# Attention and feed-forward steps on one core: ScalarE's squares put ahead of VectorE's rotation, and the Gelu, its table loads and the copies of a step reordered

## The chip, the cores and the metric

The program runs on one core of a Trainium2 chip. The metric is the device time of one execution in microseconds (us); lower is better. It is given as the median of several runs, and one further execution was taken by the profiler.

## The reference, cut to what matters

Eight sequences of 256 tokens with 128 features go through six layers of local attention and a gated feed-forward. A linear attention branch is computed once ahead of them, and the two are combined at the end. What the change touches is inside one layer:

```python
qkv = x @ Wqkv                       # 16 heads of 64
q = l2norm(q) * qs ; k = l2norm(k) * ksc
q = q * cos * scale + rotate_half(q) * sin * scale
k = k * cos * inv   + rotate_half(k) * sin * inv
sim = einsum(q, k over own and previous window of 32) * 8, masked
attn = softmax(sim) ; out = attn @ v ; x = out @ Wo + x
xn = layernorm(x) ; a, gate = split(xn @ W1 + b1)
x = (a * gelu(gate)) @ W2 + b2 + x
...
g = silu(x) ; result = x_in + s * g
```

## The kernel before, in words

The five engines run five programs written out by hand, in order, and meet at semaphores. The work is cut into 48 **steps** (`n`, one sequence of one layer) and each step into 4 **units** (`u = 4 n + j`, with `j` from 0 to 3: two groups of eight heads by two tiles of 128 tokens). The `j`-th part of a step is called **slot j** here. An iteration of the loop is software-pipelined: slot j of step n projects unit u, turns q and k of unit u-2, scores them and takes their softmax, multiplies unit u-3 with v, and does a share of the feed-forward of the sequences n-1, n-2 and n-3. Steps 0 to 2 and the three after the last are written out; the others are a loop on each engine. The same program body serves all, with `live(...)` leaving out what does not exist.

What each engine does in one slot, in its order (before the change):

- **TensorE** (lines 727 to 764): project q (three matmuls, lines 617 to 619, by the helper line 490), turn q of u-2 into `ps_qs` (line 596), project k, turn k into `ps_tk`, project v, in slot 2 the down projection `ff_down` (line 711 on), turn the probabilities of u-3 into `ps_po` (`turn_p`, line 604), the scores of u-2 (`scores`, line 621: one matmul with the mask, then 64 small ones; it waits for both `q_turned` and `k_turned`), a share of out projection or `ff_up`, and the values of u-3. A projection into `ps_q` or `ps_k` waits until the last reader of that bank is done. `ff_down` waits for `xn_ready` of the next sequence, since both use the bank `ps_f`; `ff_up` of chunk 0 waits for `x_ready`, which `after_ff` gives.
- **ScalarE** (lines 918 to 953): `keep_turned` copies q and then k out of PSUM (through the helper line 838), `squares_of` squares q and k (line 844; it waits until VectorE has rotated them), `keep_p` copies the turned probabilities in two halves, `start_norms` takes Ln and Exp of the sums of squares (lines 876 and 878), `ff_copy` takes the up projection (lines 899 and 901), then the Exp of the softmax (line 944), `keep_v` and `keep_attention`. At the end of slot 0 stands the Gelu of sequence n-3 (line 906), ahead of which the compiler puts a load of the activation table; in slot 1 `natural_log_exp_and_others` is loaded back (line 935). In the last steps `silu_start` (line 914) takes an Exp of a finished sequence, at the end of a slot.
- **VectorE** (lines 1188 to 1229): `rotate` q and `rotate` k (two tensor_tensor from PSUM each, lines 1076 and 1078), with `ln_normalise` (line 1153, gives `xn_ready`) between them in slot 2, then the two sums of squares (line 1084), `clamp` (line 1094, a tensor_scalar of 18 columns), in slot 2 `after_ff` (line 1159), `find_max` (line 1116), `newton_1` (line 1099), `less_max` (line 1121, gives `sub_done`, for which the Exp waits), `newton_2` and `newton_3` (lines 1105 and 1111), and `sums` (lines 1127 and 1130). In slot 3 `newton_2`, `newton_3` and `after_attention` (line 1135) stand ahead of `less_max`. In the last steps `silu` (lines 1173 to 1187: a chain of six operations on VectorE for a finished sequence) ends a slot.
- **GpSimd** (lines 462 to 481): `divide` for u-3 (line 433), `add_halves` for q and k (line 418, waits for each rotation), in slot 1 the gate `ff_gate` (lines 440 and 442), in slot 2 the split of a slice of weights, in slot 3 the rounding of x, then `normalise` q and k (line 426, waits for `rnorm_done` from `newton_3`).
- **SyncE** issues the loads of the weights and the shifted copies of v.

The squares and the rotation both read the projection in its PSUM bank. Before the change their order is rotation, then squares:

```python
            def squares_of(u, i, s):
                wait(act, ssq_done, 2 * (u - 2) + i + 1)
                act.wait_ge((q_scaled, k_scaled)[i], u + 1)
```

```python
                wait(dve, (tq_done, tk_done)[i], u - 1)
                wait(dve, added, u - 1)
                dve.wait_ge(done, u + 1)
```

Of the kernel before, what the change touches and what calls it, by code (L numbers as in the profile page):

```python
# [39 lines left out]
UNITS = 4  # L40
# [22 lines left out]
def build(nc, x, wq, wk, wv, wp, bp, conv_w, conv_b, wqkv, q_scale, k_scale, wo, ln_g, ln_b, w1, b1, w2,  # L63
          rotary, masks, eye, head_block, out):
    with ExitStack() as ctx:
# [422 lines left out]
        def _(pe):  # L488
# [238 lines left out]
            def body(n):  # L727
                for j in range(UNITS):
                    u = UNITS * n + j
                    for i, ps, free, done in ((0, ps_q, q_squared, q_done), (1, ps_k, k_squared, k_done)):  # L730
                        if live(u):
                            project(n, j, i, ps, free, done)

                        if live(u - 2):
                            turn_qk(u - 2, i, j % 2)
                        if i == 1 and j == 0 and live_batch(n - 2):
                            ln_mean(n - 2)
                        if i == 0 and j == 1 and live_batch(n - 2):
                            ln_variance(n - 2)
                        if i == 0 and j == 2 and live_batch(n - 2):  # L740
                            ln_spread(n, n - 2)
                        if i == 0 and j == 3 and live_batch(n - 2):
                            ff_up(n - 2, 1)
# [26 lines left out]
        def _(act):  # L770
# [69 lines left out]
            def squares_of(u, i, s):  # L840

                wait(act, ssq_done, 2 * (u - 2) + i + 1)
                act.wait_ge((q_scaled, k_scaled)[i], u + 1)
                nc.scalar.activation(squares[:, s, OCTET * i:OCTET * i + OCTET], (ps_q, ps_k)[i][:], ACT.Square  # L844
                                     ).then_inc((q_squared, k_squared)[i], 1)
# [8 lines left out]
            def keep_turned(u, j, s):  # L854

                octet, tile = j // 2, j % 2
                wait(act, s_done, u - 1)
                act.wait_ge(tq_done, u + 1)
                copy(q_t[:, s, :], ps_qs[:]).then_inc(q_turned, 1)
                act.wait_ge(tk_done, u + 1)  # L860
                copy(k_t[:, octet, :, WINDOW + P * tile:WINDOW + P * tile + P],
                     ps_tk[:].rearrange("p (c t) -> p c t", t=P)).then_inc(k_turned, 1)
# [55 lines left out]
            def body(n):  # L918
                for j in range(UNITS):
                    u = UNITS * n + j  # L920
                    if live(u - 2):
                        keep_turned(u - 2, (j - 2) % UNITS, j % 2)
                    if live(u):
                        squares_of(u, 0, j % 2)
                    if j == 0 and live(u - 3):
                        keep_p(u - 3, (j - 3) % 2)
                    if live(u):
                        squares_of(u, 1, j % 2)
                    if j > 0 and live(u - 3):
                        keep_p(u - 3, (j - 3) % 2)  # L930
# [11 lines left out]
                    if live(u - 2):  # L942
                        act.wait_ge(sub_done, u - 1)
                        nc.scalar.activation(prob[:, j % 2, :], prob[:, j % 2, :], ACT.Exp,  # L944
                                             scale=QK_SCALE).then_inc(exp_done, 1)
                    if live(u):
# [3 lines left out]
                    if j == 0 and live_batch(n - 3):  # L950
                        gelu(n - 3)
                    for b in silu_at(n, j):
                        silu_start(b)
# [5 lines left out]
        def _(dve):  # L959
# [104 lines left out]
            def rotate(n, j, i):  # L1064
# [4 lines left out]
                ps, done, scaled, added = ((ps_q, q_done, q_scaled, q_added), (ps_k, k_done, k_scaled, k_added))[i]  # L1069
                wait(dve, (tq_done, tk_done)[i], u - 1)  # L1070
                wait(dve, added, u - 1)
                dve.wait_ge(done, u + 1)
# [116 lines left out]
            def body(n):  # L1189
                for j in range(UNITS):  # L1190
                    u = UNITS * n + j
                    if live(u):
                        rotate(n, j, 0)
                    if j == 2 and live_batch(n - 2):
# [8 lines left out]
                    if live(u):  # L1203
                        sum_squares(u, 0, j % 2)
# [5 lines left out]
                    if live(u - 2):  # L1210
                        find_max(u - 2, j % 2)
                    if normed(n, j):
                        newton_1(n, j)
                    if j == 3 and normed(n, j):
# [4 lines left out]
                    if live(u - 2):  # L1219
                        less_max(u - 2, j % 2)  # L1220

                    if j != 3 and normed(n, j):
                        newton_2(n, j)
                        newton_3(n, j)
# [81 lines left out]
```

## Time and profile before

| what | value |
|---|---|
| median of 3 runs | 1858.23 us (1858.08 to 1860.93) |
| the profiled execution | 1855.56 us |
| its span in the trace | 1853.8 us |
| granted TensorE clock, mean over the span | 0.978 |
| busy share PE / DVE / ACT / POOL | 90% / 77% / 73% / 70% |
| instructions in the trace | 68588 |

PE is TensorE's matmuls and PEld its weight loads, DVE is VectorE, ACT is ScalarE, POOL is GpSimd. The span runs from the first to the last instruction of the trace; the execution's own time is 1.8 us longer, and the median of the runs is 2.7 us above that of the profiled execution. The time of one instruction in a timeline row is its duration from start to end; on PE, DVE and ACT the next one may start before that end. Matmuls are named by their output and inputs, `ps_q<-w_hi,xs_hi`.

### The profile page before, as it was taken

To read this page: it belongs to the slowest core of one execution; us is meant where nothing else is said; L and a number is where in the kernel's file an instruction comes from. 1 tells how busy PE (TensorE), PEld (TensorE's weight loads), DVE (VectorE), ACT (ScalarE), POOL (GpSimd) and SP (SyncE) were. 2 spreads that over 40 slices of the span, in tenths; PEclk is the share of its full clock that TensorE was granted. 3 is DMA by queue.
4 is the path that set the end of the run, shared out by engine and by line. 5 is a ranking of instruction groups with operands and counts; after the bars stand their busy time and mean duration, and the time that the engine had idled before them with its cause. 6 is when DMAs were issued, how large, how long until landed. Compare 5 with 4: busy or idle time off the path is not lost.

```text
span 1853.8 us, 68588 instructions
## 1 busy us (share of the span) xinstructions
PE 1663.1 (90%) x25968; PEld 1291.5 (70%) x26160; DVE 1430.3 (77%) x3041; ACT 1344.7 (73%) x2656; POOL 1293.3 (70%) x1283
## 2 busy tenths in 40 slices
PE   7889999999999999999999999999999999999973
PEld 5667777777777777677777777767777776777751
DVE  4588878878778787887778778788777777778755
ACT  4267777777777777777777777777777777777753
POOL 5287777777777777777777777777777777677720
PEclk9799999999999999999999999999999999999995
DMA  5011111111101011110111101111110111101000
GB/s 164 11 38 34 32 33 32 30 40 48 32 28 34 28 41 46 33 30 28 34 45 41 34 28 30 31 47 37 33 34 29 33 37 32 30 24 30 25 14 20
DMA packets 41406, 66.13 MB, mean 36 GB/s; under 512 B 7072, under 2 KB 16032, under 8 KB 41376
## 3 DMA queue, kind: packets, MB, share of 16 engines
q1 hardware_dynamic: 40224, 65.38, 11.7%
q10 hardware_dynamic: 1152, 0.34, 0.1%
q8 instruction: 20, 0.33, 0.1%
q14 instruction: 10, 0.08, 0.0%
HBM read 20.61 MB, written 1.05 MB: 12 GB/s over the span
## 4 chain that ended last, share of the span: by engine, by line
PE 68%; ACT 11%; issue 10%; DVE 9%; POOL 1%; ACTq 1%; DMA 0%; DVEq 0%
PE ps_a L490 11%; PE ps_f L490 11%; PE ps_qs L490 9%; PE ps_po L490 8%; PE ps_q L490 7%; PE ps_k L490 5%; PE ps_v L490 5%; PE ps_po L604 4%; PE ps_qs L596 3%; PE ps_tk L596 3%; ACT L906 2%; DVE ssq L1084 2%; DVE prob L1121 2%; ACT p_bd L838 2%; ACT squares L844 2%
## 5 line engine op out<-in xcount | busy, mean ns | idle before, releaser
L426 POOL TENSOR_TENSOR qk<-qk,rnorm 128x512 f32<-128x512 f32 x384 | 393.1, 1045 | 298.2 <-DVE rnorm L1111 298.2
L418 POOL TENSOR_TENSOR qk<-qk,qk_rot 128x512 f32<-128x512 f32 x384 | 483.7, 1276 | 111.1 <-DVE qk_rot L1078 110.8
L1084 DVE TENSOR_REDUCE ssq<-squares 128x8 f32<-128x512 f32 x384 | 257.6, 680 | 71.1 <-ACT squares L844 58.2
L490 PE MATMUL ps_qs<-k_t,q_t 64*32 64x64 f32 x12288 | 210.7, 218 | 67.6 <-ACT k_t L838 46.5
L838 ACT COPY p_bd<-ps_po 64x512 f32<-64x512 f32 x384 | 221.3, 576 | 34.7 <-PE ps_po L604 32.4
L433 POOL TENSOR_TENSOR prob<-prob,row_inv 128x512 f32<-128x512 f32 x192 | 200.3, 1043 | 51.5 <-DVE row_inv L1130 51.5
L1127 DVE TENSOR_REDUCE row_sum<-prob 128x8 f32<-128x512 f32 x192 | 131.7, 686 | 120.6 <-ACT prob L944 120.6
L490 PEld LDWEIGHTS ps_qs<-k_t,q_t 64*32 64x32 f32 x12288 | 179.7, 107 | 57.2 <-issue 57.2
L944 ACT ACTIVATE prob<-prob 128x512 f32<-128x512 f32 x192 | 121.2, 631 | 110.9 <-DVE prob L1121 107.6
L490 PEld LDWEIGHTS ps_po<-p_bd,v_back 128*64 128x64 f32 x3072 | 162.9, 137 | 49.5 <-issue 31.8
L490 PE MATMUL ps_po<-p_bd,v_back 128*64 128x64 f32 x3072 | 193.9, 225 | 1.6 <-ACT p_bd L838 1.5
L490 PE MATMUL ps_po<-p_bd,v_own 128*64 128x64 f32 x3072 | 189.5, 222 | 0.0
L490 PE MATMUL ps_a<-attn_t,wo_sb 128*64 128x257 f32 x1536 | 187.9, 386 | 0.0
L838 ACT COPY k_t<-ps_tk 128x512 f32<-128x512 f32 x192 | 112.9, 588 | 86.7 <-PE ps_tk L596 81.9
L490 PE MATMUL ps_f<-xn,w_sb 128*128 128x256 f32 (+1 forms) x576 | 160.6, 402 | 7.3 <-ACT ff_g L901 1.9
L1076 DVE TENSOR_TENSOR qk<-ps_q,table 128x512 f32<-128x512 f32 x192 | 132.6, 691 | 40.8 <-issue 29.6
L490 PEld LDWEIGHTS ps_po<-p_bd,v_own 128*64 128x64 f32 x3072 | 155.9, 138 | 0.0
L844 ACT ACTIVATE squares<-ps_k 128x512 f32<-128x512 f32 x192 | 115.2, 600 | 54.0 <-DVE qk_rot L1078 52.9
L1076 DVE TENSOR_TENSOR qk<-ps_k,table 128x512 f32<-128x512 f32 x192 | 131.0, 682 | 28.7 <-PE ps_tk L596 28.6
L604 PE MATMUL ps_po<-ident,prob 128*128 128x128 f32 x768 | 119.5, 278 | 31.0 <-POOL prob L433 31.0
L604 PEld LDWEIGHTS ps_po<-ident,prob 128*128 128x128 f32 x768 | 88.1, 140 | 82.5 <-issue 70.0
L844 ACT ACTIVATE squares<-ps_q 128x512 f32<-128x512 f32 x192 | 115.8, 603 | 40.8 <-DVE qk_rot L1078 40.7
(161 smaller groups left out, 4002.6 us busy)
## 6 DMA issues: line engine op xcount, KB each, us to landing
v_back<-v_own SPq DMA_DIRECT2D x192, 192.0 KB, 2.4
w_raw<-in_wqkv SPq DMA_DIRECT2D x48, 192.0 KB, 2.4
v_back<-v_own SPq DMA_DIRECT2D x96, 64.0 KB, 2.1
wo_sb<-in_wo SPq DMA_DIRECT2D x12, 256.0 KB, 3.0
w_sb<-in_w SPq DMA_DIRECT2D x6, 341.0 KB, 3.4
w_sb<-in_w SPq DMA_DIRECT2D x6, 192.0 KB, 2.7
x_in<-in_x SPq DMA_DIRECT2D x4, 256.0 KB, 5.0
out<-s_out SPq DMA_DIRECT2D x8, 128.0 KB, 1.9
```

The costliest lines, as they stand in the source:

```text
L418: nc.gpsimd.tensor_tensor(qk[:, s, i, :], qk[:, s, i, :], qk_rot[:, s, i, :], ALU.add).then_inc(added, 1)
L426: nc.gpsimd.tensor_tensor(heads(qk[:, s, i, :]), heads(qk[:, s, i, :]), rnorm[:, s, 8 * i:8 * i + 8].unsqueeze(2).to_broadcast([P, 8, HEAD ...
L433: nc.gpsimd.tensor_tensor(heads(prob[:, s, :]), heads(prob[:, s, :]), row_inv[:, s, :].unsqueeze(2).to_broadcast([P, 8, HEAD]), ALU.mult). ...
L490: return nc.tensor.matmul(o, lhs, rhs, start=start, stop=stop, **kw)
L596: last = nc.tensor.transpose(ps[:, P * c:P * c + P], qk[:, s, i, P * c:P * c + P], ident[:])
L604: last = nc.tensor.transpose(ps_po[:, P * c:P * c + P], prob[:, s, P * c:P * c + P], ident[:])
L838: return nc.scalar.copy(o, i)
L844: nc.scalar.activation(squares[:, s, OCTET * i:OCTET * i + OCTET], (ps_q, ps_k)[i][:], ACT.Square).then_inc((q_squared, k_squared)[i], 1)
L944: nc.scalar.activation(prob[:, j % 2, :], prob[:, j % 2, :], ACT.Exp, scale=QK_SCALE).then_inc(exp_done, 1)
L1076: V.tensor_tensor(heads(qk[:, s, i, :]), heads(ps[:]), cos.unsqueeze(1).to_broadcast([P, 8, HEAD]), ALU.mult)
L1084: V.tensor_reduce(ssq[:, s, 8 * i:8 * i + 8], heads(squares[:, s, OCTET * i:OCTET * i + OCTET]), AX, ALU.add).then_inc(ssq_done, 1)
L1127: V.tensor_reduce(row_sum[:, s, :], heads(prob[:, s, :]), AX, ALU.add).then_inc(sum_done, 1)
```

## The change

`squares_of` no longer waits for VectorE's rotation but for the projection itself, and VectorE's rotation waits for the squares; the projection's bank is then free when the rotation is done, so TensorE waits for `q_scaled` and `k_scaled` in place of `q_squared` and `k_squared`. On ScalarE `keep_turned` is cut in two: the order at the head of a slot becomes squares of q, copy of q of u-2, (in slot 1 the Gelu,) squares of k, copy of k of u-2, and `keep_p` stands behind them in every slot. The Gelu moves from the end of slot 0 into slot 1, and its table is loaded by an explicit instruction behind the Exp of slot 0, ahead of `keep_v` and `keep_attention`. `silu_start` moves ahead of that load and of both copies. On VectorE the sum of squares of q stands right behind the rotation of q, `less_max` right behind `find_max`, and the three newton operations behind it in every slot.

```diff
--- before.py
+++ after.py
@@ -727,7 +727,7 @@
             def body(n):
                 for j in range(UNITS):
                     u = UNITS * n + j
-                    for i, ps, free, done in ((0, ps_q, q_squared, q_done), (1, ps_k, k_squared, k_done)):
+                    for i, ps, free, done in ((0, ps_q, q_scaled, q_done), (1, ps_k, k_scaled, k_done)):
                         if live(u):
                             project(n, j, i, ps, free, done)
 
@@ -840,7 +840,7 @@
             def squares_of(u, i, s):
 
                 wait(act, ssq_done, 2 * (u - 2) + i + 1)
-                act.wait_ge((q_scaled, k_scaled)[i], u + 1)
+                act.wait_ge((q_done, k_done)[i], u + 1)
                 nc.scalar.activation(squares[:, s, OCTET * i:OCTET * i + OCTET], (ps_q, ps_k)[i][:], ACT.Square
                                      ).then_inc((q_squared, k_squared)[i], 1)
 
@@ -851,12 +851,15 @@
                 act.wait_ge(v_done, u + 1)
                 copy(v_own[:, j, :], ps_v[:]).then_inc(v_copied, 1)
 
-            def keep_turned(u, j, s):
-
-                octet, tile = j // 2, j % 2
+            def keep_turned_q(u, s):
                 wait(act, s_done, u - 1)
                 act.wait_ge(tq_done, u + 1)
                 copy(q_t[:, s, :], ps_qs[:]).then_inc(q_turned, 1)
+
+            def keep_turned_k(u, j):
+
+                octet, tile = j // 2, j % 2
+                wait(act, s_done, u - 1)
                 act.wait_ge(tk_done, u + 1)
                 copy(k_t[:, octet, :, WINDOW + P * tile:WINDOW + P * tile + P],
                      ps_tk[:].rearrange("p (c t) -> p c t", t=P)).then_inc(k_turned, 1)
@@ -918,15 +921,17 @@
             def body(n):
                 for j in range(UNITS):
                     u = UNITS * n + j
-                    if live(u - 2):
-                        keep_turned(u - 2, (j - 2) % UNITS, j % 2)
                     if live(u):
                         squares_of(u, 0, j % 2)
-                    if j == 0 and live(u - 3):
-                        keep_p(u - 3, (j - 3) % 2)
+                    if live(u - 2):
+                        keep_turned_q(u - 2, j % 2)
+                    if j == 1 and live_batch(n - 3):
+                        gelu(n - 3)
                     if live(u):
                         squares_of(u, 1, j % 2)
-                    if j > 0 and live(u - 3):
+                    if live(u - 2):
+                        keep_turned_k(u - 2, (j - 2) % UNITS)
+                    if live(u - 3):
                         keep_p(u - 3, (j - 3) % 2)
                     if j == 0 and live_batch(n - 2):
                         ln_square(n - 2)
@@ -943,14 +948,15 @@
                         act.wait_ge(sub_done, u - 1)
                         nc.scalar.activation(prob[:, j % 2, :], prob[:, j % 2, :], ACT.Exp,
                                              scale=QK_SCALE).then_inc(exp_done, 1)
+                    for b in silu_at(n, j):
+                        silu_start(b)
+                    if j == 0 and live_batch(n - 3):
+
+                        nc.scalar.preload_act_table_set("gelu_and_others")
                     if live(u):
                         keep_v(u, n, j)
                     if live(u - 3):
                         keep_attention(u - 3, n if j >= 3 else n - 1, (j - 3) % UNITS)
-                    if j == 0 and live_batch(n - 3):
-                        gelu(n - 3)
-                    for b in silu_at(n, j):
-                        silu_start(b)
 
             iterations(act, body)
 
@@ -1066,10 +1072,10 @@
                 u = UNITS * n + j
                 s = j % 2
                 tile = j % 2
-                ps, done, scaled, added = ((ps_q, q_done, q_scaled, q_added), (ps_k, k_done, k_scaled, k_added))[i]
+                ps, squared, scaled, added = ((ps_q, q_squared, q_scaled, q_added), (ps_k, k_squared, k_scaled, k_added))[i]
                 wait(dve, (tq_done, tk_done)[i], u - 1)
                 wait(dve, added, u - 1)
-                dve.wait_ge(done, u + 1)
+                dve.wait_ge(squared, u + 1)
                 at = n // BATCHES * (4 * TILES * HEAD) + (2 * i * TILES + tile) * HEAD
                 cos = table[:, span(at, HEAD)]
                 sin = table[:, span(at + TILES * HEAD, HEAD)]
@@ -1191,6 +1197,7 @@
                     u = UNITS * n + j
                     if live(u):
                         rotate(n, j, 0)
+                        sum_squares(u, 0, j % 2)
                     if j == 2 and live_batch(n - 2):
                         ln_normalise(n - 2)
                     if live(u):
@@ -1201,7 +1208,6 @@
                     if j == 1 and live_batch(n - 2):
                         ln_var(n - 2)
                     if live(u):
-                        sum_squares(u, 0, j % 2)
                         sum_squares(u, 1, j % 2)
                     if normed(n, j):
                         clamp(n, j)
@@ -1209,19 +1215,13 @@
                         after_ff(n - 3)
                     if live(u - 2):
                         find_max(u - 2, j % 2)
+                        less_max(u - 2, j % 2)
                     if normed(n, j):
                         newton_1(n, j)
-                    if j == 3 and normed(n, j):
                         newton_2(n, j)
                         newton_3(n, j)
                     if j == 3 and live_batch(n - 1):
                         after_attention(n - 1)
-                    if live(u - 2):
-                        less_max(u - 2, j % 2)
-
-                    if j != 3 and normed(n, j):
-                        newton_2(n, j)
-                        newton_3(n, j)
                     if live(u - 2):
                         sums(u - 2, j % 2)
                     if isinstance(n, int) and n == 0 and j == 0:
```

## Rows read from the trace of the kernel before

**Rows 1.** The page, parts 1 and 5: busy time of the engines; one group.

```profile
PE 1663.1 (90%) x25968; PEld 1291.5 (70%) x26160; DVE 1430.3 (77%) x3041; ACT 1344.7 (73%) x2656; POOL 1293.3 (70%) x1283
...
L1084 DVE TENSOR_REDUCE ssq<-squares 128x8 f32<-128x512 f32 x384 | 257.6, 680 | 71.1 <-ACT squares L844 58.2
```

**Rows 2.** Waits of TensorE, 400 to 1400 us: total us, times, longest us.

```profile
PE ps_qs L490 <- ACT k_t L838: 28.0, 28, 1.0
PE ps_po L604 <- POOL prob L433: 15.9, 28, 0.6
```

**Rows 3.** Timeline of TensorE, slots 0 to 2 of one step: start us, duration us.

```profile
987.66 0.49 PE L490 MATMUL ps_q<-w_hi,xs_hi 128*128 x1
...
988.22 0.40 PE L490 MATMUL ps_q<-w_hi,xs_lo 128*128 x1
...
989.36 0.39 PE L490 MATMUL ps_k<-w_hi,xs_lo 128*128 x1
...
999.81 0.63 PE L604 MATMUL ps_po<-ident,prob 128*128 128x128 f32 x4 [0.57 <-POOL prob L433]
...
1001.44 1.10 PE L490 MATMUL ps_qs<-k_t,q_t 64*32 64x64 f32 x64 [1.00 <-ACT k_t L838]
...
1005.28 0.50 PE L490 MATMUL ps_q<-w_hi,xs_hi 128*128 x1
...
1009.05 1.52 PE L490 MATMUL ps_f<-ff_m,w_sb 128*64 128x257 f32 x12
...
1012.51 1.13 PE L490 MATMUL ps_f<-xn,w_sb 128*128 128x256 f32 x4
```

**Rows 4.** Timeline of ScalarE, the same step, end of slot 0 and slot 1.

```profile
996.27 0.63 ACT L944 ACTIVATE prob<-prob 128x512 f32<-128x512 f32 x1
...
997.89 1.28 ACT L906 ACT_TABLE_LOAD   x1
...
999.18 0.85 ACT L906 ACTIVATE ff_g<-ff_g 128x768 f32<-128x768 f32 x1
...
1000.40 0.59 ACT L838 COPY k_t<-ps_tk 128x512 f32<-128x512 f32 x1
...
1000.87 0.61 ACT L844 ACTIVATE squares<-ps_q 128x512 f32<-128x512 f32 x1
```

**Rows 5.** Timeline of VectorE, the same step, slots 0 to 2.

```profile
990.30 0.69 DVE L1076 TENSOR_TENSOR qk<-ps_q,table 128x512 f32<-128x512 f32 x1 [0.66 <-issue]
...
994.66 0.18 DVE L1094 TENSOR_SCALAR ssq_c<-ssq 128x18 f32<-128x18 f32 x1
...
995.55 0.69 DVE L1121 TENSOR_TENSOR prob<-ps_qs,row_max 128x512 f32<-128x512 f32 x1
...
1002.83 0.56 DVE L1094 TENSOR_SCALAR ssq_c<-ssq 128x18 f32<-128x18 f32 x1
...
1007.19 0.69 DVE L1076 TENSOR_TENSOR qk<-ps_q,table 128x512 f32<-128x512 f32 x1
...
1008.40 0.48 DVE L1153 SCALAR_TENSOR_TENSOR xn<-ps_f,g_sb,xc 128x256 f32<-128x256 f32 x1
...
1011.92 0.42 DVE L1159 TENSOR_TENSOR x_run<-x_mid,ps_f 128x257 f32 x1
```

**Rows 6.** Timeline of GpSimd, the same step, slots 0 and 1.

```profile
991.67 2.51 POOL L418 TENSOR_TENSOR qk<-qk,qk_rot 128x512 f32<-128x512 f32 x2 [0.91 <-DVE qk_rot L1078]
...
1002.08 1.28 POOL L440 TENSOR_TENSOR ff_m<-ff_a,ff_g 128x512 f32<-128x512 f32 x1
```

**Rows 7.** Timeline of ScalarE and VectorE, the last 70 us of the span.

```profile
1812.64 1.28 ACT L906 ACT_TABLE_LOAD   x1
...
1814.80 1.28 ACT L914 ACT_TABLE_LOAD   x1
...
1816.09 0.84 ACT L914 ACTIVATE squares<-x_run 64x256 f32<-64x256 f32 x2
...
1816.97 0.29 DVE L1176 TENSOR_SCALAR squares<-squares 128x256 f32<-128x256 f32 x1 [5.51 <-ACT squares L914]
```

## The prediction

> **What bounds the kernel now.** I read the busy shares first: TensorE is busy 90% of the span, the others 70 to 77% [rows 1]. So only what makes TensorE wait counts. Its waits over 1000 us come next: two kinds carry nearly all of it, each 28 times, so one step lasts 1000 / 28 = 35.7 us [rows 2]. Once per step the scores wait 1.0 us for the copy of k, and the turn of the probabilities waits 0.57 us for GpSimd's division. Both sit in slot 1 [rows 3]. The timeline of ScalarE shows why: the softmax's Exp, the copies of v and attention, a table load (1.28), the Gelu (0.85), the copy of q and at last the copy of k stand in one line, from 996.27 to 1000.99, and the scores begin 0.45 later [rows 4]. Two smaller places follow in slot 2. The down projection starts 0.17 after `xn` is written (1008.88), and chunk 0 of the up projection starts 0.17 after `x_run` is written (1012.34) [rows 3, 5]. Slots 0 and 3 show no such wait: there VectorE is late, but off the path.
>
> The last 70 us are another stage: VectorE works through the finished sequences in one serial chain, and stands 5.51 us until ScalarE's Exp arrives [rows 7].
>
> **Slot 0 and 1, the scores.** The q projection of slot 0 ends 0.96 us after the slot begins, at 988.62 [rows 3]. Today VectorE starts rotating at 990.30, held by the preceding slot's late softmax and by 0.66 us of issue at the head of the loop [rows 5]. In the new order `less_max` of slot 3 stands ahead of two other jobs, so VectorE is free sooner, and the squares (0.61 [rows 4]) let the rotation begin at 988.62 + 0.61 + 0.08 of handing over = 989.3, 1.0 earlier. From there to `less_max` (995.55 today [rows 5]) the wait for the squares goes (58.2 us over 192 slots, 0.3 each [rows 1]) and `newton_1` leaves the place ahead (0.2, the length of the free clamp). Against that I set 0.33 for the clamp, see below. Exp of slot 0 starts 1.0 + 0.3 + 0.2 - 0.33 = 1.2 earlier. The squares of k wait for nothing, since that projection ends 1.13 after that of q [rows 3] and the two rotations of q take 1.2 [rows 5]. But between that Exp and the copy of k two squares are new, 0.49 each. The load, the Gelu and the copies are the same instructions in another order. The copy of k ends 1.2 - 0.98 = 0.2 earlier, so the scores and the rest of slot 1 gain **0.2 us a step**. The division is late by less than the copy is and stays hidden; if that cover went, its 0.57 would be the wait.
>
> **Slot 2, the down projection.** Rotation of q starts 1.91 after the slot begins (1007.19 less 1005.28 [rows 3, 5]). It would start at 0.96 + 0.61 + 0.08 = 1.65. Then, new, the sum of squares of q (0.68 [rows 1], of which 0.6 counts, as the two rotations of 0.69 ahead of `xn` take 1.21 together [rows 5]) stands ahead of `xn`. So `xn` and `ff_down` come 0.6 - 0.26 = 0.35 later. `after_ff` then is no longer late: the wait for the squares of k ahead of it is gone, and 0.17 of it comes back at the up projection. Net **0.15 to 0.2 lost a step**.
>
> **The rest of a step.** Slot 0 and 3: no TensorE wait to remove; the copies of q and k and the turned probabilities have slack there, at no cost. That `keep_p` now always follows the squares of k costs nothing: the values matmuls stand behind another group of TensorE work. TensorE's waits for the banks now end with the second rotation, over 3 us before the next slot's projection. SyncE's order is unchanged; the shifted copies of v start behind `keep_v`, now 1.28 behind the load, but are used three slots later. GpSimd's gate waits for the Gelu, which by the line above ends about 0.2 earlier than today (two squares and a copy now stand ahead of it, and the Exp 1.2 earlier). Sum of the steady steps: 45 x (-0.2 + 0.17) = -1 to -2 us.
>
> **The last steps.** `silu_start` moves ahead. At 1812.64 a Gelu load, the Gelu, a second load back (1.28) and only then the Exp of a finished sequence run, at 1816.09 [rows 7]. In the new order the Exp comes first, at 1812.64: 3.45 earlier, below the 5.51 that VectorE waits, and VectorE's chain from there to the end is serial. The Exps of the first two finished sequences also move ahead of an attention copy (0.5 to 0.6 each, [rows 4]), and `less_max` ahead of `newton_1` adds some of it: 1 to 2 us more on the same chain. Sum: -3.5 to -5.5, taken -5.
>
> **Total:** -2 - 5 = -7 us. Against the profiled execution (1855.56 us, with 1.8 outside its span) that is 1848.5; the median of the runs stands 2.7 above it, so 1858.2 - 7 = 1851.
>
> **The operation the trace shows only in part** is the clamp under GpSimd. The same 18 columns take 0.18 in slot 0, while GpSimd idles, and 0.56 in slot 1 [rows 5], ending at 1003.39 just after GpSimd's gate product ends at 1003.36 [rows 6]. So it stands until GpSimd's instruction is over. Today it comes late enough to miss the halves' additions (1.26 each [rows 6]); in the new order the sum of squares no longer waits, and the clamp falls into the middle of the second addition. Bounds: 0 if it slips by, 0.33 if it waits for that one, 1.28 if the gate's first product gets in ahead. I take 0.33, since in slot 1 today it got in between the two gate products.
>
> The Trainium skill, SBUF — State Buffer, "Who interferes with whom", says that a VectorE instruction in a two-port mode, or with two inputs in SBUF, shares an interface with GpSimd and that whoever issued first keeps it for the whole instruction. By that rule the newton operations (two small SBUF inputs) are held too, and in slot 1 they would now meet the gate. It speaks against the change: without any such holding a step would gain another 0.2 to 0.3; with all of it, rival C below.
>
> **Rivals.**
> - **B, the steady steps do gain** (15%). If the clamp is not held, Exp of slot 0 is 0.33 earlier, and with it the copy of k: 45 x 0.3 = 14 us more, 1837 to 1842. For it: the wait for k is the largest one. Against: the 0.56 of the clamp.
> - **C, slower** (20%). Place: slot 1, between the sums of squares and the rotation of slot 2. The gate (two products, 1.28 and then a shorter one) starts when the additions are over, just when the clamp and then the newton operations come. If the clamp loses its turn, max, `less_max`, Exp and the sum of probabilities all slip 1.28; VectorE has about 0.3 us of slack before the rotation in slot 2. It decides from there: 0.6 us or more late means `xn` late and TensorE idle, 45 x 0.6 = 27 less 7, so 1870 to 1880. A mild form, in which rotation of q in slot 2 merely starts as late as now (1.91), costs 0.26 a step: 45 x 0.26 - 7 = +5, 1863. For it: 0.35 of the loss in slot 2 is certain. Against: today's clamp got its turn.
> - **D, nothing** (15%). The steady steps balance or lose 0.1, and the chain of the last steps is held elsewhere (by the out projection behind the later attention copy): 1855 to 1862. Here belongs that the change does not do what it says: were a second load put ahead of the Gelu, 45 x 1.28 = 58 us would be lost; the copies and squares already run between Gelu and load back without one, so 1 in 50.
> - **A, the forecast** (50%): 1846 to 1856.
>
> **How the numbers follow.** 0.2%, or 3.7 us, is about what a measurement of this kernel can tell from no change. Faster: nearly all of A (0.45) and B (0.15) = 0.60. Same: the upper edge of A and most of D = 0.18. Slower: C and the rest of D = 0.22. The range reaches down to 1838, into B, and up to 1866, over C's mild form; it leaves out half of B and half of C. A alone would be 1846 to 1856.
>
> **What would show it.** Still one wait of about 0.8 us for the copy of k per step, beginning near the same place; no wait for `less_max`. The Gelu 35.6 to 35.7 us apart. In slot 2 the down projection some 4.1 us behind the slot's first matmul, not 3.77. VectorE's wait for ScalarE's squares at the sums gone, but the clamp over 0.3 us in every slot but few. No L914 table load, and the 5.5 us wait in the last steps below 2. Wrong would be: Gelus under 35.4 apart (B), over 35.9 (C), or a chain of the last steps as long as now (D).

## The result: 3.9% slower, and the profile after

| | before | after |
|---|---|---|
| median | 1859.34 us (4 runs, 1858.08 to 1860.93) | 1929.30 us (4 runs, 1928.01 to 1940.55) |
| profiled execution, its span | 1855.56, 1853.8 | 1930.52, 1928.7 |
| granted clock, mean | 0.978 | 0.944 |

The ratio is 1.0391, with a 95% interval of 1.0364 to 1.0418. The forecast was 1851, its range 1838 to 1866.

The page of the changed kernel, parts 1, 2 and 5 (the row PEclk is the granted TensorE clock of 40 slices of the span in tenths; the last part of a group's row is its idle time and what ended it):

```profile
PE 1760.5 (91%) x26160; PEld 1341.8 (70%) x26160; DVE 1485.8 (77%) x3041; ACT 1345.4 (70%) x2655; POOL 1301.7 (67%) x1283
...
PEclk8799999999999999999999999999999999999996
...
L418 POOL TENSOR_TENSOR qk<-qk,qk_rot 128x512 f32<-128x512 f32 x384 | 489.9, 1276 | 286.4 <-DVE qk_rot L1084 285.5
...
L1082 DVE TENSOR_TENSOR qk<-ps_q,table 128x512 f32<-128x512 f32 x192 | 132.8, 692 | 243.0 <-ACT squares L844 242.9
```

TensorE is busy 97 us longer than before [rows 1] with the same matmuls. Part of that is only in the records: the 192 mask matmuls have none in the trace of before (25968 matmuls against 26160), and e9 below, with all records and no low clock in its steady steps, is busy 1706.5 us, 43 more than before. The rest goes with the granted clock, which is lower. The row PEclk hardly shows it: from the third slice to the last but one it reads 9 as it did before, but 9 stands for 90% or more. In stretches of 400 us the mean was 0.95 to 0.97, and 1.00 before. Ahead of the rotations VectorE now waits 243 us for ScalarE's squares, a wait that did not exist, and GpSimd 286 us for VectorE's rotation.

Waits of TensorE, 400 to 1400 us, as in [rows 2]:

```profile
PE ps_qs L490 <- ACT k_t L838: 39.5, 27, 1.5
PE ps_f L490 <- DVE xn L1159: 10.6, 27, 0.4
PE ps_po L604 <- POOL prob L433: 5.5, 27, 0.2
```

The timeline of TensorE in slots 1 and 2 of a step, to be held against [rows 3]:

```profile
970.22 0.63 PE L604 MATMUL ps_po<-ident,prob 128*128 128x128 f32 x4 [0.20 <-POOL prob L433]
...
972.32 0.38 PE L490 MATMUL ps_qs<-mask_b,ident_b 128*128 128x512 bf16 x1 [1.47 <-ACT k_t L838]
...
972.62 1.93 PE L490 MATMUL ps_qs<-k_t,q_t 64*32 64x64 f32 x64
...
974.49 2.71 PE L490 MATMUL ps_a<-attn_t,wo_sb 128*64 128x257 f32 x16
...
978.06 0.50 PE L490 MATMUL ps_q<-w_hi,xs_hi 128*128 x1
...
982.15 1.52 PE L490 MATMUL ps_f<-ff_m,w_sb 128*64 128x257 f32 x12 [0.39 <-DVE xn L1159]
...
985.43 1.13 PE L490 MATMUL ps_f<-xn,w_sb 128*128 128x256 f32 x4
```

The turn of the probabilities ends at 970.85 and the next matmul starts at 972.32. TensorE stands for 1.47 us in one piece. Before, slot 1 had three pieces: 0.27 at the turn of q, 0.57 at the turn of the probabilities and 0.69 ahead of the scores (the 1.00 of [rows 2] less the 0.31 of the mask matmul, which has no record there). Then the 64 score matmuls take 1.93 (1.10 before) and the out projection 2.71 (1.96 before).

Granted clock in consecutive stretches of 2 us, same place (columns: stretch, its length, busy time of PE, PEld, DVE, ACT and POOL, granted clock, DMA share, GB/s):

```profile
970.53:972.53 2.00, 0.53 (x4) 0.18 (x2) 2.00 (x4) 2.00 (x4) 1.03 (x1) 1.00 0.18 57
972.53:974.53 2.00, 2.00 (x67) 1.74 (x66) 1.97 (x5) 1.95 (x3) 1.47 (x2) 0.53 0.00 0
974.53:976.53 2.00, 2.00 (x16) 1.24 (x14) 1.84 (x4) 0.80 (x3) 1.95 (x3) 0.62 0.00 0
976.53:978.53 2.00, 2.00 (x42) 1.66 (x37) 1.15 (x4) 1.15 (x3) 1.51 (x2) 1.00 0.00 0
```

Right behind the standstill the clock is at its lower level, 1.2 GHz: (1 - 0.53) / 0.5 x 2 + (1 - 0.62) / 0.5 x 2 = 3.4 us of it. Such a stretch is called a **fall** here.

Timeline of ScalarE, slot 1, and the Gelus of three more steps, to be held against [rows 4]:

```profile
967.12 1.28 ACT L955 ACT_TABLE_LOAD   x1
...
969.38 0.61 ACT L844 ACTIVATE squares<-ps_q 128x512 f32<-128x512 f32 x1
...
970.33 0.88 ACT L909 ACTIVATE ff_g<-ff_g 128x768 f32<-128x768 f32 x1
...
971.08 0.62 ACT L844 ACTIVATE squares<-ps_k 128x512 f32<-128x512 f32 x1
...
971.56 0.62 ACT L838 COPY k_t<-ps_tk 128x512 f32<-128x512 f32 x1
...
1007.88 0.88 ACT L909 ACTIVATE ff_g<-ff_g 128x768 f32<-128x768 f32 x1
...
1532.19 0.88 ACT L909 ACTIVATE ff_g<-ff_g 128x768 f32<-128x768 f32 x1
...
1568.34 0.88 ACT L909 ACTIVATE ff_g<-ff_g 128x768 f32<-128x768 f32 x1
```

From 970.33 to 1007.88 a step lasts 37.55 us, from 1532.19 to 1568.34 it lasts 36.15. Of the 44 intervals between the first and the last Gelu of the regular steps, 37 are of the first kind and 7 of the second; the difference, 1.40 us, goes with a fall: each of the 37 has one, none of the 7 has.

Timeline of VectorE, slots 1 and 2, against [rows 5]:

```profile
970.13 0.69 DVE L1082 TENSOR_TENSOR qk<-ps_q,table 128x512 f32<-128x512 f32 x1 [2.07 <-ACT squares L844]
...
973.92 0.69 DVE L1100 TENSOR_SCALAR ssq_c<-ssq 128x18 f32<-128x18 f32 x1
...
976.05 0.47 DVE L1105 SCALAR_TENSOR_TENSOR rn_a<-ssq_c,rn 128x18 f32<-128x18 f32 x1
...
979.70 0.69 DVE L1082 TENSOR_TENSOR qk<-ps_q,table 128x512 f32<-128x512 f32 x1 [1.93 <-ACT squares L844]
...
981.50 0.47 DVE L1159 SCALAR_TENSOR_TENSOR xn<-ps_f,g_sb,xc 128x256 f32<-128x256 f32 x1
...
983.79 0.76 DVE L1100 TENSOR_SCALAR ssq_c<-ssq 128x18 f32<-128x18 f32 x1
```

VectorE stands 2.07 us ahead of the rotation of q in slot 1, since the squares of q (969.38) are behind the table load and two copies. The clamps take 0.69 and 0.76, and the first of the newton operations 0.47.

**The sum.** The spans differ by 74.9 us. The 44 steps give 71.7: 44 x (36.15 - 35.70) = 19.8 and 37 x 1.40 = 51.8. The stretch ahead of the first Gelu is 6.4 longer (184.54 against 178.09), with 41 us at the low clock against 27. The clock alone does not explain this: in e1 that stretch has 27 us at the low clock too, and lasts 183.7. The stretch behind the last regular Gelu is 3.2 shorter (101.7 against 104.9).

### The profile page after: what moved, and what is told of

The parts are those of the page before. It is cut to its first block, busy times and chain, and to the rows that moved or that the text cites. A ratio compares the mean times of both kernels' runs of the same rounds, so it can differ in the third digit from the quotient of the medians.

```text
span 1928.7 us, 68969 instructions
## 1 busy us (share of the span) xinstructions
PE 1760.5 (91%) x26160; PEld 1341.8 (70%) x26160; DVE 1485.8 (77%) x3041; ACT 1345.4 (70%) x2655; POOL 1301.7 (67%) x1283
## 4 chain that ended last, share of the span: by engine, by line
PE 77%; ACT 9%; DVE 8%; issue 5%; POOL 1%; DVEq 0%; DMA 0%; ACTq 0%
PE ps_qs L490 14%; PE ps_a L490 13%; PE ps_f L490 12%; PE ps_po L490 10%; PE ps_q L490 8%; PE ps_k L490 5%; PE ps_qs L596 4%; PE ps_po L604 4%; ACT squares L844 3%; PE ps_v L490 3%; DVE qk_rot L1084 2%; PE ps_tk L596 2%; DVE ssq L1090 1%; DVE xn L1159 1%; ACT k_t L838 1%
## 5 line engine op out<-in xcount | busy, mean ns | idle before, releaser
L418 POOL TENSOR_TENSOR qk<-qk,qk_rot 128x512 f32<-128x512 f32 x384 | 489.9, 1276 | 286.4 <-DVE qk_rot L1084 285.5
L490 PEld LDWEIGHTS ps_qs<-k_t,q_t 64*32 64x32 f32 x12288 | 209.3, 119 | 57.5 <-issue 57.5
L490 PE MATMUL ps_qs<-k_t,q_t 64*32 64x64 f32 x12288 | 243.4, 236 | 0.0
L490 PE MATMUL ps_a<-attn_t,wo_sb 128*64 128x257 f32 x1536 | 217.3, 431 | 0.0
L490 PEld LDWEIGHTS ps_a<-attn_t,wo_sb 128*64 128x64 f32 x1536 | 115.4, 157 | 70.3 <-issue 29.7
L1122 DVE TENSOR_REDUCE row_max<-ps_qs 128x8 f32<-128x512 f32 x192 | 131.3, 684 | 40.1 <-PE ps_qs L490 39.5
L1127 DVE TENSOR_TENSOR prob<-ps_qs,row_max 128x512 f32<-128x512 f32 x192 | 132.8, 692 | 14.5
L838 ACT COPY attn_t<-ps_po 128x512 f32<-128x512 f32 x192 | 114.9, 598 | 32.5 <-PE ps_po L490 32.5
```

What stands on the lines that cost most here:

```text
L418: nc.gpsimd.tensor_tensor(qk[:, s, i, :], qk[:, s, i, :], qk_rot[:, s, i, :], ALU.add).then_inc(added, 1)
L490: return nc.tensor.matmul(o, lhs, rhs, start=start, stop=stop, **kw)
L838: return nc.scalar.copy(o, i)
L1122: V.tensor_reduce(row_max[:, s, :], heads(ps_qs[:]), AX, ALU.max).then_inc(max_done, 1)
L1127: V.tensor_tensor(heads(prob[:, s, :]), heads(ps_qs[:]), row_max[:, s, :].unsqueeze(2).to_broadcast([P, 8, HEAD]), ALU.subtract).then_inc( ...
```

## The experiments

Two questions: what lets the clock fall, and what costs the 0.45 us in a step without a fall. "Standstill" is how long TensorE stands directly ahead of the mask matmul of slot 1, from the timeline; where that matmul has no record, 0.31 is taken off the wait ahead of the score matmuls, in a step without a fall. The falls are counted over the 44 regular intervals of the profiled execution.

| kernel | median us | ratio to before (95%) | standstill | step without / with a fall | falls |
|---|---|---|---|---|---|
| before | 1859 | 1 | 0.69 | 35.70 | 0 |
| after | 1929.3 | 1.0391 (1.0364 to 1.0418) | 1.47 | 36.15 / 37.55 | 37 |
| e1 | 1872.4 | 1.0059 (1.0033 to 1.0085) | 0.74 | 36.13 | 0 |
| e2 | 1879.4 | 1.0100 (1.0069 to 1.0130) | 1.46 | 35.75 / 37.15 | 15 |
| e3 | 1944.1 | 1.0443 (1.0409 to 1.0477) | 1.66 | 36.95 / 37.6 to 37.9 | 33 |
| e4 | 1942.3 | 1.0443 (1.0416 to 1.0471) | 1.63 | 36.65 / 37.6 to 38.0 | 33 |
| e5 | 1873.8 | 1.0085 (1.0057 to 1.0113) | at most 0.61 | 36.15 | 0 |
| e6 | 1804.3 | 0.9707 (0.9683 to 0.9730) | none | 34.61 | 0 |
| e7 | 1853.2 | 0.9971 (0.9955 to 0.9986) | 0.69 | 35.72 | 0 |
| e8 | 1832.6 | 0.9862 (0.9834 to 0.9890) | 0.47 | 35.15 | 0 |
| e9 | 1824.5 | 0.9803 (0.9776 to 0.9830) | 0.49 | 35.16 | 0 |
| e10 | 1822.5 | 0.9795 (0.9765 to 0.9826) | none | 35.03 | 0 |
| e11 | 1798.1 | 0.9659 (0.9632 to 0.9686) | none | 34.52 | 0 |
| e12 | 1943.3 | 1.0439 (1.0403 to 1.0475) | 1.22 | 36.2 / 37.55 | 42 |

**e1, the Gelu behind the copy of k** (edit of the changed kernel):

```diff
-                    if j == 1 and live_batch(n - 3):
-                        gelu(n - 3)
                     if live(u):
                         squares_of(u, 1, j % 2)
                     if live(u - 2):
                         keep_turned_k(u - 2, (j - 2) % UNITS)
+                    if j == 1 and live_batch(n - 3):
+                        gelu(n - 3)
```

> The changed kernel with one move: in slot 1 the Gelu stands behind the copy of k instead of ahead of it. Theory (T): the 1.47 us for which TensorE stands in one piece ahead of the scores, waiting for the copy of k, is what the clock falls after. The copy of k ends 0.75 earlier, the gap shrinks to about 0.7, the clock stays up in all steady steps: step 36.15 - 0.75 = 35.4 us, total about 1929 - 52 (clock) - 34 = 1843. Rival (X): the clock falls because of the late xn in slot 2 (0.39 us of waiting): then the falls stay, total about 1895.

No fall of the clock is left, so the scores' standstill is tied to it and the wait for `xn` is not: that wait grew to 0.67 a step in this run. But the step is 36.13, not 35.4. The timeline of TensorE shows a wait that the expectation had left out:

```profile
979.30 1.10 PE L490 MATMUL ps_qs<-k_t,q_t 64*32 64x64 f32 x64 [1.05 <-ACT k_t L838]
...
980.96 1.96 PE L490 MATMUL ps_a<-attn_t,wo_sb 128*64 128x257 f32 x16 [0.56 <-DVE ssq L1151]
```

The scores start 0.7 earlier and the out projection then waits 0.56 for `ssq`, which is `ln_var`. It stands behind both rotations on VectorE, and these are late.

**e2, `xn` first in slot 2** (edit of the changed kernel):

```diff
                         rotate(n, j, 0)
-                        sum_squares(u, 0, j % 2)
+                    if live(u) and j != 2:
+                        sum_squares(u, 0, j % 2)
                     if j == 2 and live_batch(n - 2):
                         ln_normalise(n - 2)
+                    if live(u) and j == 2:
+                        sum_squares(u, 0, j % 2)
```

> The changed kernel with one move: in slot 2 the sum of squares of q stands behind ln_normalise (xn), as before the change; elsewhere it stays ahead. T: xn is 0.6 earlier, the wait of 0.39 ahead of ff_down goes, a step loses 0.35 to 0.5 (about 20 us in all), but the clock still falls behind the scores' gap in most steps: 1905 to 1912. X: the clock stays up, 1929 - 52 - 18 = 1859.

The 0.40 a step came back (36.15 to 35.75), as T had it, and 1.40 more with a fall as before. Falls became rarer, 15 instead of 37, with the same standstill, which neither T nor X had, and the total, 1879.4, lies between the two. So a standstill of this length does not bring the clock down each time. Whether it does is not random either: in e2 the falls come in five groups of three steps in a row with four gaps of five to seven steps between them, and in the changed kernel 33 steps in a row have one, the next five none.

**e3, the squares ahead of the rotation alone** (the kernel before, with the diff's lines on `q_scaled`, `q_done`, `squared`, and ScalarE's order at the head of a slot; Gelu, `silu_start` and VectorE's order of before):

> The kernel before with one part of the change alone: squares ahead of the rotation, the copies of q and k interleaved with them, keep_p behind; Gelu at the end of slot 0, VectorE's order as before. T: the two squares stand ahead of the copy of k (+0.98) and the Exp of slot 0 comes only some 0.3 to 0.6 earlier, so the gap ahead of the scores grows to 1.5 to 2 us and the clock falls: step 36.1 to 36.6 without and 1.4 more with a fall, total 1920 to 1950. Rival (Y), that VectorE's new order (sum of squares of q early, less_max early) is the culprit: 1855 to 1862.

The swap by itself costs 1.25 us a step (36.95 against 35.70) where T had 0.4 to 0.9, and brings 33 falls, one in all but every fourth step. Its median is 15 us above that of the whole change, though the two intervals touch.

**e4 and e12, a dose in the kernel before**: a copy that nothing reads, of 1024 columns (e4) or 512 (e12), ahead of the copy of k in slot 1. The edit of e4; in e12 the copy is `lnt[:, 4:6, :]` from `lnt[:, 2:4, :]`:

```diff
                 copy(q_t[:, s, :], ps_qs[:]).then_inc(q_turned, 1)
+                if j == 3:
+                    nc.scalar.copy(linear[:, TOKENS:5 * TOKENS], x_in[:, 0:4 * TOKENS])
                 act.wait_ge(tk_done, u + 1)
```

> The kernel before with a suspected cost added: one copy of 1024 columns on ScalarE (about 1.0 us) in slot 1 between the copies of q and of k; nothing reads it. T: the gap ahead of the scores grows from 1.0 to about 2.0, a step by 1.0, and the clock falls in most steps, 1.4 each: 1858 + 45 + 50 = 1950 to 1965. Rival (Z), that the clock has nothing to do with this gap: 1858 + 45 = 1903.

> The kernel before with a further copy of 512 columns (0.47) instead of e4's 1024 between the copies of q and k of slot 1; nothing reads it. The standstill ahead of the scores is 0.47 longer, about 1.5 with the mask's part, near that of the changed kernel. T: a step of 36.15 to 36.2 without a fall, and falls in a part of the steps, 1.4 each: 1890 to 1930. Rival (Z): the clock falls only above some longer standstill, all steps 36.2, 1878 to 1882.

Both bring the clock down in the kernel before, which has nothing of the change in it. e4 came out 8 to 23 below its expectation: every fourth step, 11 of 44, has no fall, and a fall costs 1.0 to 1.3 there. Of the 33 falls, 22 begin while TensorE still stands in e3 and 12 in e4. In e12 the wait of slot 1 is (timeline of TensorE):

```profile
1009.44 0.38 PE L490 MATMUL ps_qs<-mask_b,ident_b 128*128 128x512 bf16 x1 [1.22 <-ACT k_t L838]
```

1.22 us in one piece, and 42 of 44 steps have a fall; the total is above what was expected (1890 to 1930), because half a microsecond of delay brought nearly as many falls as could be. e12's copy holds ScalarE for 0.52 us a step and costs 82 us: 22 for the delay, 42 x 1.3 = 55 with the falls, and the rest outside the 44 steps.

**e5, the gap filled with useless matmuls** (edit of the changed kernel):

```diff
                         turn_p(u - 3, (j - 3) % 2)
+                    if j == 1 and live_batch(n - 3):
+                        pe.wait_ge(ff1_copied, FF_N * (n - 2))
+                        for _ in range(4):
+                            mm(ps_f[:], ident_b[:], mask_b[:, 0, :], True, True)
```

> The changed kernel with useless work in the gap: in slot 1, between the turn of the probabilities and the scores, TensorE runs four matmuls with the mask (128x512, 0.31 us each by the rows of the changed kernel) into a bank that is idle then; nothing reads them. The gap ahead of the scores shrinks from 1.47 to about 0.3 with nothing any earlier. Theory (T), that the clock falls behind one long standstill of TensorE: no fall in the steady steps, all of them 36.15, total 1929 - 52 = 1877. Rival (V), that it falls for something else in slot 1 or 2 (the load of all engines, xn's wait): the falls stay, 1925 to 1930.

```profile
977.90 0.63 PE L604 MATMUL ps_po<-ident,prob 128*128 128x128 f32 x4 [0.20 <-POOL prob L433]
...
978.58 0.81 PE L490 MATMUL ps_f<-mask_b,ident_b 128*128 128x512 bf16 x3
...
980.00 0.38 PE L490 MATMUL ps_qs<-mask_b,ident_b 128*128 128x512 bf16 x1 [0.61 <-ACT k_t L842]
```

With the fill behind the turn (978.58) and nothing earlier, the longest piece is at most 0.61 (one of the four useless matmuls has no record), all 44 steps are 36.15, and the total falls by 55 us to 1873.8. The falls of the clock are thus caused by the standstill itself and cost 52 to 55 us; the other 15 us of the loss stay. (1873.8 lies in the range that rival C of the prediction had, 1870 to 1880. Its last link is there, a late `xn`, but not its cause, so the match is luck.)

**e6 and e10, load and Gelu behind the copy of k.** e10 is the changed kernel with this edit alone. e6 has also `ln_var` ahead of the rotation of k in slot 1, and e2's edit:

```diff
                         keep_turned_k(u - 2, (j - 2) % UNITS)
+                    if j == 1 and live_batch(n - 3):
+                        nc.scalar.preload_act_table_set("gelu_and_others")
+                        gelu(n - 3)
...
-                    if j == 0 and live_batch(n - 3):
-
-                        nc.scalar.preload_act_table_set("gelu_and_others")
```

> The changed kernel with the table load and the Gelu together behind the copy of k of slot 1, ln_var ahead of the rotation of k in slot 1, and the sum of squares of q behind xn in slot 2. T: ScalarE's line ahead of the copy of k loses 1.28 + 0.75 = 2.0 us, the squares of q in slot 1 start with the projection, VectorE's rotation in slot 1 2 us earlier, no wait of TensorE over 0.5, no fall of the clock: step 33.8 to 34.6, total 1790 to 1825, below both kernels. Rival (W): the switch of tables now stands ahead of keep_p and start_norms, rnorm of slot 1 comes late and the work for slot 2 waits instead: 35.5 to 36, 1850 to 1870.

> The changed kernel with only the table load and the Gelu moved behind the copy of k of slot 1 (e6 without its two moves on VectorE). T: no standstill ahead of the scores, no fall of the clock; of e6's 34.6 us it lacks xn's earlier place (0.4 to 0.6 in slot 2) and perhaps ln_var's (the out projection waits up to 0.5 in slot 1): step 34.9 to 35.5, total 1815 to 1845. Rival (U): the moves on VectorE did most of e6, total 1860 or more.

Both beat the kernel before. ScalarE in e6 (timeline, slot 1):

```profile
973.05 0.61 ACT L844 ACTIVATE squares<-ps_q 128x512 f32<-128x512 f32 x1
...
974.48 0.62 ACT L838 COPY k_t<-ps_tk 128x512 f32<-128x512 f32 x1
...
975.12 1.28 ACT L934 ACT_TABLE_LOAD   x1
...
976.42 0.84 ACT L909 ACTIVATE ff_g<-ff_g 128x768 f32<-128x768 f32 x1
```

The squares of q now directly follow the copy of the attention; the load and the Gelu stand behind the copy of k and ahead of the copies of the turned probabilities, which only the slot's last matmuls need. Slot 1 takes 8.7 us instead of 10.2. e10 shows that this move does nearly all (35.03), and the two moves on VectorE 0.42 (34.61). In e10 TensorE stands in slot 2 instead, in each of the 44 steps:

```profile
961.29 1.52 PE L490 MATMUL ps_f<-ff_m,w_sb 128*64 128x257 f32 x12 [0.98 <-DVE xn L1158]
```

That is 0.98 us in one piece, and no fall follows. The rival W was right in a small part: the rotation of q in slot 2 starts 2.2 to 2.3 behind the slot's first matmul, later than before (1.91), and the step, 34.61, came out at the upper end of what T had (33.8 to 34.6).

**e7, only the Exps of finished sequences ahead** (kernel before; `silu_start` behind the Exp of the softmax):

> The kernel before with silu_start moved ahead of keep_v, keep_attention and the Gelu, and nothing else. By the prediction's term for the last steps: the steady steps stay 35.70, the stretch behind the last regular Gelu shrinks from 104.9 by 3.5 to 5.5, total 1853 to 1855. Rival (D): the last chain is held elsewhere and stays.

The steady steps stay (35.72), the last stretch shrinks from 104.9 to 99.0, the median by 5.2 of 1858.4. The prediction's term for this part, 3.5 to 5.5, was nearly right.

**e8, `less_max` ahead of the newton operations alone** (kernel before, with the diff's lines on this):

> The kernel before with VectorE's new order of less_max and the newton operations alone. Exp of slot 0 comes 0.2 earlier (newton_1 no longer ahead), so the copy of k 0.2 earlier and a step is 35.5: 1848 to 1852. Rival (Y), that this order is part of the loss (newton operations later, rnorm late, divisions late): over 1860.

0.55 us a step, not 0.2: 35.15, the ratio 0.9862. Waits of TensorE, 400 to 1400 us:

```profile
PE ps_qs L490 <- ACT k_t L838: 22.0, 28, 0.8
PE ps_po L604 <- POOL prob L433: 21.9, 28, 0.8
```

The wait for the copy of k (0.8 in place of 1.0) is the part that was expected. The other is in slot 2. `less_max` and hence the Exp and the sums of slot 1 end earlier, the rotation of q starts 1.52 behind the slot's first matmul instead of 1.91, `xn` comes 0.4 earlier, and both short waits of slot 2 go (9.03 us for the slot against 9.37).

**e9, the change without the swap** (squares wait for the rotation again, TensorE for the squares, ScalarE's order of before with the Gelu between the copies of q and k of slot 1; early load, `silu_start` and VectorE's order of `less_max` as changed):

> The change with one part undone: the squares wait for the rotation again, and the order on the three engines is that of before where it hangs on this (copy of q, copy of k, squares; both sums of squares behind both rotations). The Gelu between the copies of q and k of slot 1, its early table load, silu_start ahead and VectorE's order of less_max and newton stay. Theory (T): the swap alone is the loss; without it the step is that of e8 (35.15 us; load and Gelu stand ahead of the copy of k as before), the clock does not fall, and the last steps give 4 more: 1826 to 1830. Rival (U): the moved load or Gelu costs something of its own, 1850 or more.

1824.5 us, the step of e8, no fall. Of all parts of the change the swap (with the order of the copies and of the sum of squares of q that goes with it) alone makes it slow: 1929.3 - 1824.5 = 105 us, 44 x (36.15 - 35.16) = 44 of them in every step and 52 by the clock. Of the rest, 5 are in the last stretch (96.6 against 101.7) and 2 ahead of the first Gelu. The moved load and Gelu cost and bring nothing.

**e11, a version that takes what the runs pointed to.** Squares first in slot 1 alone, there with `ln_var` ahead of the rotation of k as in e6:

```diff
+                    if j == 1:
+                        if live(u):
+                            squares_of(u, 0, j % 2, True)
+                        if live(u - 2):
+                            keep_turned_q(u - 2, j % 2)
+                        if live(u):
+                            squares_of(u, 1, j % 2, True)
+                        if live(u - 2):
+                            keep_turned_k(u - 2, (j - 2) % UNITS)
+                        if live_batch(n - 3):
+                            nc.scalar.preload_act_table_set("gelu_and_others")
+                            gelu(n - 3)
...
-                dve.wait_ge(done, u + 1)
+                dve.wait_ge((q_squared, k_squared)[i] if j == 1 else done, u + 1)
```

> A version that takes what each run pointed to: squares ahead of the rotation in slot 1 alone, where ScalarE would otherwise wait, rotation first in slots 0, 2 and 3; load and Gelu behind the copy of k of slot 1; less_max ahead of the newton operations; ln_var ahead of the rotation of k; silu_start ahead. T: slot 1 as in e6 (8.7), slot 2 as in e8 (9.0), the others unchanged: step 33.8 to 34.1, total 1765 to 1785. Rival (W): the late switch of tables makes the norms of slot 1 late and slot 2 waits: 34.6 or more, 1800 and up.

1798.1 us, 3.4% below the kernel before, the lowest median of all (0.09 us a step below e6), though 0.4 to 0.7 us a step above what was expected and nearly at rival W's numbers. Its only wait of TensorE:

```profile
PE ps_po L604 <- POOL prob L433: 22.7, 29, 0.8
```

Slot 2 is 9.08 as in e8, but slot 1 is 9.34, not 8.7: the turn of the probabilities waits 0.8 us for GpSimd's division, since in slot 0, with rotation first, the sums of squares and `rnorm` are later than in e6 (1.28 against 0.62 behind the start of slot 1). GpSimd normalises and divides behind that. No run has the swap in slots 0 and 1 alone.

## Why the prediction was wrong

- **The missing case: the clock.** 52 of the 75 us are granted clock. The prediction held TensorE's clock for given, and no rival had it. Its own numbers contained the warning: it took the waits ahead in slot 1 as gone or hidden and left "one wait of about 0.8 us for the copy of k". But if the copy of k ends at the same time and the pieces ahead of it vanish, their time goes into the last piece: 0.27 + 0.57 + 0.69 = 1.53 before, 0.20 + 1.47 = 1.67 after. Filling that piece takes the falls away (e5), lengthening it brings them into the kernel before (e4, e12). The sum over a step is not: it is 0.20 + 0.74 + 0.56 + 0.67 = 2.17 in e1 without a fall, and 0.20 + 1.46 = 1.66 in e2 with 15. Whether it is the length of the one piece or the idle time within slot 1 (1.53 before and 1.50 in e1 without a fall, 1.66 and more with falls) no run tells apart.
- **Slots 0 and 1, "the copy of k ends 0.2 earlier": it ends 0.1 later.** With slot 2 below this is why even a step without a fall is 0.45 longer (0.1 and 0.34). The chain from the Exp of slot 0 to the copy of k is 5.70 long as worked out (4.72 + 0.98). The Exp came 0.88 earlier, not 1.2 (7.73 behind slot 0's first matmul, 8.61 before): the rotation of slot 0 started at 1.82, not 1.65, as the softmax of slot 3 still ended late on VectorE (its reciprocal 1.03 behind the start of slot 0) and the head of the loop takes its time behind that, 0.66 in [rows 5]. From that rotation to `less_max` it took 5.18 instead of 5.25, 0.07 less where 0.3 + 0.2 - 0.33 = 0.17 was taken.
- **Slot 2, "0.15 to 0.2 lost": 0.34 lost.** In the steps without a fall the rotation of q started 1.84 behind the slot's first matmul, not 1.65: ScalarE's squares are behind the attention copy of a late slot 1 and came 1.19 behind the slot's start. So `ff_down` came at 4.28 instead of 3.77, 0.51 late and not 0.35. The 0.17 did come back: `x_run` was written at 6.60, as before, the up projection no longer waits for it, and 0.51 - 0.17 = 0.34 remains.
- **The clamp: right in kind.** 0.43, 0.69, 0.76 and 0.76 in the four slots, each until GpSimd's second addition is over, where 0.18 + 0.33 = 0.51 was taken. By the rule of the Trainium skill (SBUF — State Buffer, "Who interferes with whom") the newton operations should be held too, and the trace agrees in slot 1: `rn_a` took 0.47 there beside the gate's last product, 0.17 in the others. Rival C's step, the clamp losing its turn to the gate, did not happen; 0.69 is its time beside the addition alone.
- **What the swap displaced.** The prediction saw that VectorE starts on the squares; it did not price the start in slot 1, where the squares are behind the table load: rotation of q 4.0 behind the slot's first matmul, 2.86 before and 2.63 in e9. `ln_var`, behind the rotations, became the out projection's wait as soon as the scores were earlier (e1).
- **`less_max` ahead: the sign right, the size less than half** (0.2 against 0.55, e8). The rest of the gain lay a slot later.
- **The last steps: right but for the edges.** -3.2 in the change, -5.9 alone (e7), where -3.5 to -5.5 was forecast. The wait of 5.51 [rows 7] is 1.93 in the changed kernel, "below 2" as forecast, and the L914 table load is gone.

Open: why e2, with the same standstill as the changed kernel (1.46), had 15 falls instead of 37, and where the falls begin. The longest piece that no fall followed is 0.98 us (e10, in slot 2; ahead of the mask matmul 0.74, in e1), the shortest with falls 1.22 (e12). Open too is what the swap itself brings in e6, e10 and e11. No run has the load and the Gelu behind the copy of k without it, and e10, with the swap, is as fast as e9, without the swap and that move (1822.5 and 1824.5).

## What to carry to other kernels

Before a wait is priced by its end, draw TensorE's idle pieces of the stage with their lengths: removing the early ones while the last releaser stays put gains nothing, and here it went with a lower clock. Where an engine that was waited for last (ScalarE here, by a table load and a Gelu) gets more work ahead of the waiting result, the swap has to come with the move of something else behind that result; the same swap with load and Gelu moved behind the copy of k is 2% faster than before (e10), and without that move 3.9% slower. And undo or add the parts one by one: this change held a part worth -1.4% (e8), one worth -0.3% (e7), and one worth +4.4% by itself (e3).

## What was not expected of the hardware

A standstill of TensorE of 1.2 to 1.7 us, once in 36 to 38 us, with the engine 87 to 91% busy over the span, was enough to bring the granted clock to 1.2 GHz for 3.4 us, in 15 (e2) to 42 (e12) of 44 steps. The fall began between 0.4 us ahead of the standstill's end (e3, e4) and 0.9 behind it (e2). With no piece over 0.98 us (e10) there was none. A fall cost 1.4 us of the step in the changed kernel, and 0.7 to 1.3 in e3, e4 and e12. Four useless matmuls of 0.3 us each in the gap, which delayed nothing, removed all of them (e5).
